# Mixture-of-experts stage of a decoder: turned combination weights copied next to their turning, the routing's exponential at the head of its iteration, the routing in pieces, another tail

## The reference

```python
logits = jnp.einsum('btc,ce->bte', x, router_w) + router_b        # 8 experts
top_k_logits, expert_indices = jax.lax.top_k(logits, 2)
expert_probs = jax.nn.softmax(top_k_logits, axis=-1)
# each token's place in its expert's buffer: a running count over the tokens,
# first choices before second choices; capacity 38 per sequence and expert
einp = buf.at[ei.ravel(), pos.ravel()].add(xr)
h = jnp.einsum('eti,eih->eth', einp2, w_c_fc) + b_c_fc            # 128 -> 512
g = jnp.einsum('eti,eih->eth', einp2, w_gate) + b_gate
o = jnp.einsum('eth,eho->eto', jax.nn.silu(h * g), w_c_proj) + b_c_proj
sel = o[i, p]
return jnp.sum(pr[..., None] * sel, axis=1)                       # two choices, weighted
```

## Time and profile before

| | |
|---|---|
| median of 3 runs | 2416.77 us (2414.82 to 2422.31) |
| the profiled execution: its time / its span | 2416.03 us / 2414.1 us |
| busy share of the span: PE, DVE, ACT, POOL | 76%, 72%, 63%, 51% |
| granted TensorE clock over the span | 0.875 of 2.4 GHz |
| this stage, first `hidden` to the end | 1785.4 to 2414.1 us |

### The profile page before, as it was taken

The page is one execution under the profiler, slowest core; times in us unless marked ns, Lnnn a source line. Parts: engine busy times, 40 slices in busy tenths (PEclk is TensorE's granted clock), DMA queues, the critical chain, the costliest instruction groups (busy, mean ns, idle before and its releaser), DMA issues. The chain is left out here.

```text
span 2414.1 us, 51135 instructions
## 1 busy us (share of the span) xinstructions
PE 1843.7 (76%) x16165; PEld 1336.3 (55%) x16174; DVE 1733.8 (72%) x4027; ACT 1510.8 (63%) x2647; POOL 1236.7 (51%) x1186
## 2 busy tenths in 40 slices
PE   3777777799999824444677499999868898888888
PEld 2556555466666612222345377777646666666665
DVE  5889995689888689998566378888655555545553
ACT  1788886577777645554465477877535556556554
POOL 2656664588888757877666378888610000000000
PEclk7799998699999955555888699999979999999999
DMA  4000000101010030000000000000000000000000
GB/s 137 2 0 0 0 1 2 41 22 31 21 31 21 5 104 1 0 0 1 1 0 0 14 7 8 8 8 1 1 1 10 0 9 9 9 0 9 9 9 9
DMA packets 63117, 32.46 MB, mean 13 GB/s; under 512 B 27737, under 2 KB 59569, under 8 KB 63025
## 3 DMA queue, kind: packets, MB, share of 16 engines
q1 hardware_dynamic: 60576, 30.42, 4.7%
q10 hardware_dynamic: 2448, 0.90, 0.2%
HBM read 27.12 MB, written 4.19 MB: 13 GB/s over the span
## 5 line engine op out<-in xcount | busy, mean ns | idle before, releaser
L3174 DVE SCALAR_TENSOR_TENSOR m_z<-psum,bias_col,m_hb 128x304 f32<-128x304 f32 x256 | 134.4, 532 | 206.8 <-ACT m_hb L3030 199.8
L182 POOL TENSOR_SCALAR mln_ve<-mln_mv 128x4 f32<-128x4 f32 x16 | 4.5, 280 | 484.7 <-DVE mln_mv L149 484.7
L3030 ACT ACTIVATE m_hb<-psum,bias_col 128x304 f32<-128x304 f32 x256 | 130.7, 511 | 171.8 <-PE psum L2929 171.2
L2929 PE MATMUL psum<-m_xt,w_fc 128*128 128x304 f32 x512 | 175.5, 424 | 4.5 <-ACT m_xt L3022 4.5
L1412 POOL TENSOR_TENSOR x_gated<-x_score,x_gate 128x1232 f32<-128x1232 f32 x64 | 168.5, 2632 | 12.7 <-ACT x_score L1347 9.6
L2932 PE MATMUL psum<-m_xt,w_gate 128*128 128x304 f32 x512 | 174.9, 423 | 0.0
L2941 PE MATMUL psum<-m_hid,w_proj 128*128 128x304 f32 x512 | 171.4, 421 | 0.0
L470 POOL TENSOR_SCALAR_AFFINE_SELECT a_prob<-a_prob 128x1024 f32<-128x1024 f32 x128 | 137.5, 1096 | 54.7 <-ACT a_prob L515 54.0
L1354 ACT COPY x_pT<-psum 77x512 f32<-77x512 f32 x256 | 135.8, 581 | 44.8 <-PE psum L1225 43.4
L1419 POOL TENSOR_TENSOR x_gated<-x_gated,x_rden 128x1232 f32<-128x1232 f32 x64 | 143.8, 2247 | 35.8 <-DVE x_rden L1498 30.7
L509 ACT ACTIVATE a_prob<-psum 128x1024 f32<-128x1024 f32 x128 | 129.6, 1029 | 50.3 <-PE psum L619 29.8
(11 more groups left out here) (408 smaller groups left out, 5644.3 us busy)
## 6 DMA issues: line engine op xcount, KB each, us to landing
x_ctx<-in_ctx_dram SPq DMA_DIRECT2D x32, 154.0 KB
x_mask<-in_mask_BxSxS_ik_dram SPq DMA_DIRECT2D x64, 77.0 KB, 2.6
x_resident<-in_x_dram SPq DMA_DIRECT2D x8, 512.0 KB, 7.0
out_dram<-x_resident SPq DMA_DIRECT2D x8, 512.0 KB, 3.2
x_gate<-in_fside_BxSxS_dram SPq DMA_DIRECT2D x16, 154.0 KB, 2.5
w_fc<-in_L_ffn_w_c_fc_dram SPq DMA_DIRECT2D x1, 2048.0 KB, 9.2
w_gate<-in_L_ffn_w_gate_dram SPq DMA_DIRECT2D x1, 2048.0 KB, 14.2
const<-in_const_dram SPq DMA_DIRECT2D x1, 607.0 KB, 6.1
```

The costliest lines, as they stand in the source:

```text
L2929: pe.matmul(psum[:, 2 + k % 2, 0:N * K], core.w_fc[:, e, f * P:(f + 1) * P], rhs, start=True, stop=True).then_inc(sem["h_ps"], PER_STEP)
L3030: act.activation(hb[:, k % 2, :], psum[:, 2 + k % 2, 0:N * K], ACT.Identity, bias=bias[:, fcb + k:fcb + k + 1]).then_inc(sem["h"], PER_STEP)
L3174: dve.scalar_tensor_tensor(out=z[:, k % 2, :], in0=psum[:, 4 + k % 2, 0:N * K], scalar=bias[:, gb + k:gb + k + 1], in1=hb[:, k % 2, :], op ...
```

## The change

Nothing of the arithmetic changes. On ScalarE, `combine_copy(n)` moves from k = 4n + 6, behind `expert_out`, to k = 4n + 4; the exponential moves from k = 24 of the iteration before to the very start of its own iteration; in the tail `slots_copy` runs two sequences ahead of where it was. On TensorE, `dispatch` for sequences 0 and 1 stands ahead of the tail's first `turn_rows`, and the others follow two sequences earlier. On VectorE, `combine(0)` moves from ahead of z(0) to ahead of z(1); the three operations on probabilities move from `finish` to a function of their own behind z(0); statistics are made in two halves, behind z of k = 2 and 3; normalising stands at k = 5 and 6; `choose` is split into `best` (k = 21) and `choose` (k = 22), and `finish` into `finish` (k = 29) and `keys` (k = 30); six instead of four `slots` stand ahead of the first addition. The helper `statistics_of` was there before.

```diff
@@ TensorE, iteration @@
+                if ahead:
+                    dispatch(i + STEP, 0)
+                    dispatch(i + STEP, 1)
                 pe.wait_ge(sem["oT"], i + STEP)
...
                     ins.then_inc(sem["y_ps"], BATCH)
-                    if ahead:
-                        dispatch(i + STEP, n)
+                    if ahead and n + 2 < N:
+                        dispatch(i + STEP, n + 2)
@@ ScalarE, iteration @@
+                chosen_exp(i)
                 first(0)
                 for k in range(STEPS):
                     if k + 1 < STEPS:
                         first(k + 1)
                     silu(k)
+                    if k % NF == 0 and k:
+                        combine_copy(k // NF - 1)
                     if k % NF == 2 and k > NF:
                         expert_out(k // NF - 1)
-                        combine_copy(k // NF - 1)
                     if ahead and k in (10, 14):
                         input_copy(i + STEP, (k - 10) // NF)
-                    if ahead and k == 24:
-                        chosen_exp(i + STEP)
                 expert_out(E - 1)
+                if ahead:
+                    slots_copy(i + STEP, 0)
                 combine_copy(N - 1)
...
+                if ahead:
+                    slots_copy(i + STEP, 1)
                 rows_copy(0)
                 for n in range(N):
                     if n + 1 < N:
                         rows_copy(n + 1)
-                    if ahead:
-                        slots_copy(i + STEP, n)
+                    if ahead and n + 2 < N:
+                        slots_copy(i + STEP, n + 2)
@@ VectorE @@
+            def probabilities(i):
+                prob_chain.start(i)
+                dve.wait_ge(sem["eexp"], i + STEP)
+                prob_chain.link(dve, dve.tensor_scalar(diff[:], ex[:], 1.0, None, ALU.add))
+                prob_chain.link(dve, dve.reciprocal(prob[:, 0, :], diff[:]))
+                prob_chain.last(dve, dve.tensor_tensor(prob[:, 1, :], ex[:], prob[:, 0, :], ALU.mult))
...
                 for k in range(STEPS):
-                    if k % NF == 0:
+                    if k == 1:
+                        combine(0)
+                    if k % NF == 0 and k:
                         combine(k // NF)
...
-                    if ahead and k == 1:
-                        statistics(i + STEP)
-                    if ahead and k in (4, 6):
-                        normalise(i + STEP, (k - 4) // 2)
-                    if ahead and k == 20:
+                    if k == 0:
+                        probabilities(i)
+                    if ahead and k in (2, 3):
+                        statistics(i + STEP, k - 2)
+                    if ahead and k in (5, 6):
+                        normalise(i + STEP, k - 5)
+                    if ahead and k == 21:
+                        best(i + STEP)
+                    if ahead and k == 22:
                         choose(i + STEP)
                     if ahead and k == 29:
                         finish(i + STEP)
+                    if ahead and k == 30:
+                        keys(i + STEP)
                 for s in range(STREAMS):
                     if ahead:
-                        for n in range(s * QUAD, (s + 1) * QUAD):
+                        for n in ((0, 1, 2, 3, 4, 5), (6, 7))[s]:
                             slots(i + STEP, n)
```

More of the change, by code:

```diff
@@ L2844, in moe @@
         chain = Chain(core, "m_chain", STEP)
+        prob_chain = Chain(core, "m_prob_chain", STEP)
         xn = core.sb("m_xn", [P, N, C])
@@ L3072, in iteration @@
                         rows_copy(n + 1)
-                    if ahead:
-                        slots_copy(i + STEP, n)
+                    if ahead and n + 2 < N:
+                        slots_copy(i + STEP, n + 2)
             input_copy(1, 0)
             input_copy(1, 1)
-            chosen_exp(1)
             for n in range(N):
@@ L3095, in _, with statistics, best @@
             link = lambda ins: chain.link(dve, ins)
-            def statistics(i):
-                ln.statistics(dve, i, lambda s, b: core.x_cols(i, s, b))
+            def statistics(i, s):
+                ln.statistics_of(dve, i, s, lambda b: core.x_cols(i, s, b))
             def normalise(i, s):
                 ln.apply(dve, i, s, lambda b: core.x_cols(i, s, b), lambda b: xn[:, s * QUAD + b, :], sem["xn"])
-            def choose(i):
+            def best(i):
                 chain.start(i)
@@ L3115, in choose @@
                 dve.tensor_tensor(diff[:], top[:, :, 1], top[:, :, 0], ALU.subtract).then_inc(sem["diff"], STEP)
+            def choose(i):
                 for n in range(N):
@@ L3138, in finish, with keys @@
                 link(dve.tensor_scalar(idxf[:], idxf[:], float(K), None, ALU.mult))
+            def keys(i):
                 link(dve.tensor_scalar(over[:], pos[:], float(K), -4.0 * P * E, ALU.is_ge, ALU.mult))
@@ L3191, in iteration @@
                     dve.tensor_tensor(x, x, psum[:, 1, :], ALU.add).then_inc(sem["x_out"], UNIT)
-            statistics(1)
+            for s in range(STREAMS):
+                statistics(1, s)
             for s in range(STREAMS):
                 normalise(1, s)
+            best(1)
             choose(1)
             finish(1)
+            keys(1)
             for n in range(N):
```

## The result

The changed kernel takes 2345.91 us, the median of 4 runs (2342.82 to 2346.61), beside 2415.80 for the kernel before in the same comparison (4 runs, 2412.98 to 2422.31). The ratio is 0.9705, with a 95% interval of 0.9683 to 0.9726. The forecast was 2346.5.

A forecast was written before the change was run, and what follows sets the result against it. TensorE was taken to set the time. Terms 68.1 + 8.8 - 9.4 + 0.8 + 1.6 = 69.9 us off 2416.03 gave 2346.1, stated as 2346.5 us; range 2341 to 2351 (68%), widened to 2336 to 2360.

The forecast's parts named there:

- The copies' place: Turnings on TensorE no longer wait for the copy to m_ct: 8.77 us in each of 7 iterations, -68.1 us in all.
- the head: At an iteration's start, TensorE waits for z behind VectorE's moved work: +1.1 us an iteration, +9.4 us in all.
- I cost all these cuts at nothing.: Cutting choose and finish into smaller blocks on VectorE was taken to cost nothing.
- The tail: Last projection's end to next hidden(0): dispatches fill waits, -1.25 us in each of 7 iterations, -8.8 us; 13.6 us left.
- Table loads: Exp's load at the head takes 1.28 us, hidden by the tail; the skill's 2.7 us rule would add some 10 us.
- Ahead of the loop: Before the loop, halved statistics let GpSimd start the first routing 0.8 us earlier: -0.8 us.
- The clock: In the seventh iteration, a stretch of TensorE at 1.2 GHz goes with the 2 us wait before it: -1.6 us.
- the fall at each head: Rival: TensorE's clock falls once in each iteration, after the head's new wait; +13 us, 2359 us; chance 10%.
- the half clock in the tails: Rival: TensorE stays at 1.2 GHz through every tail, 91 us more, 2437 us; chance 3%.
- The turning's wait: Rival: turnings wait on as before; only the surplus of two long waits goes, 14.4 us, giving 2401 us; chance 4%.
- The head was not free: Answers the rival that the head costs nothing because VectorE catches up: 9 us more gained, 2337 us; chance 7%.
- A matrix was late once: Answers the rival that the tail's second dispatch waits up to 0.9 us for its matrix in 7 iterations: 2352 us; 7%.

The follow-up runs named there:

- e2: The changed kernel with combine_copy(n) put back behind expert_out at k = 4n + 6, all else as changed; 2405.37 us, ratio 0.9948.
- e5: The changed kernel with finish and keys in one block behind z(29) again; 2345.58 us, ratio 0.9706, iteration 69.69 us.
- e1: The kernel before with only combine_copy(n) moved to k = 4n + 4; 2358.59 us, ratio 0.9748, iteration 71.17 us.
- e6: e4 with the exponential back at k = 24 of the iteration before and the probabilities back ahead of finish; 2347.48 us, iteration 69.71 us.
- e9: e4 with only the exponential back at k = 24 of the iteration before; 2342.76 us, ratio 0.9692, iteration 69.27 us.
- e4: The changed kernel with combine(0) ahead of z(2), second half of statistics and normalising placed later; 2334.74 us, ratio 0.9659, iteration 68.68 us.

## Why the prediction was right

*The copies' place.* Right in mechanism, place and size. The kernel lost 8.77 us an iteration there by the starts of the earlier trace rows, and no turning waits in the changed kernel. e2 gives the same from the other side, 54.5 us for 56 waits. The loop's gain, 9.15 us an iteration, is 0.2 above my sum. Behind each of the seven waits the turning itself ran 0.01 to 0.02 slower, which I left out, and the 0.17 behind `choose` (under e5) went as well. The last iteration gave 6.0; forecast were 6.7 less the head's 1.1, 5.6.

*"I cost all these cuts at nothing."* True of `finish` (e5), nearly so of `choose`, and the sum needed no more. But the reason that I gave, that ScalarE and VectorE have room on the average, was too easy. e1 shows that the copies alone bring 7.7 an iteration, not 8.8: once TensorE doesn't pause, two table loads, `combine(7)` and `finish` within five steps come through to the last projections. The exponential's and the probabilities' new places are what keeps the 8.77 whole: by e6 and e9, on top of e4, they are worth 0.59 and 0.44. I had seen their cost (the head) and took their gain for part of the sixth wait. The changed kernel's total doesn't depend on which is right, and to that extent its agreement is luck; e1 and e6 depend on it, and there I was wrong by up to 1.1 and 1.0 us an iteration.

*The tail.* 13.64 against a forecast of 13.6. `turn_rows` is 0.17 late instead of 0.83, and no wait for `m_xt` is left in the loop. The matrix for the second dispatch comes out just in time, as forecast, but for the first tail, where it costs 0.32; e9 shows the same in every tail, 0.42 us late.

*The head.* z(1) at h + 4.01 (forecast 4.0), `hidden(3)` at h + 4.60 (4.6), late by 1.02 (0.9 and restart), `hidden(6)` late by 0.23 (0.15); in the first iteration the recorded wait is 0.52 longer (0.6). The first period is 0.84 longer than the others; most of the rest is the late matrix of its tail. The head is a price that the change need not pay: e4 takes 1.01 of it away.

*Table loads.* The page ScalarE: Activation LUTs of the Trainium skill (Rules for kernel authors) would have put 2.7 us on a switch. The section What ACT_TABLE_LOAD costs, which the prediction sets against it, does not differ: its 1283 ns is the load alone, and a drain brings it to 2.66 us. This trace shows the load and no drain: a row of 1.28 us from 1926.53, and the exponential at 1927.83. The load at the head starts 0.81 us before h and lets `first(0)` start at h + 0.72; by the rule, as an estimate from that page, it would have been over a microsecond later. The stage has the 16 loads of the forecast:

```profile
L3022 ACT ACT_TABLE_LOAD x8 | 10.3, 1283 | 0.1
L3041 ACT ACT_TABLE_LOAD x8 | 10.3, 1283 | 0.1
```

*Ahead of the loop.* From the first statistics to the first `hidden(0)` it was 1757.09 to 1785.41, 28.32 us, and is 1759.57 to 1787.13, 27.56: 0.76 less (0.8). The row that does it, GpSimd's first inverse root, starts 1.84 us behind the first statistics where it started 2.61 behind:

```profile
1759.57 0.87 DVE L155 BATCH_NORM_STATS2 mln_stats<-x_resident 128x6 f32<-128x128 f32 x4 [3.09 <-PEq L71]
...
1761.41 1.04 POOL L184 TENSOR_TENSOR mln_rstd<-mln_ve,minus_half 128x4 f32<-128x4 f32 x1
```

*The clock.* The stretch at 1.2 GHz of the earlier trace rows is gone, as forecast. Whether the 2 us wait caused it stays open: seven waits of that length stood in the same trace, and one was followed by such a stretch. None of the twelve traces of kernels without that wait shows one in the loop.

*The rivals.* No window of the loop shows the lower clock, so neither the fall at each head nor the half clock in the tails came. For the latter I had cited the Trainium skill's page TensorE: Matmul & The Clock Gate (PE-mode transpose). The tails lie in windows with a granted clock of 1.00; but this is a weak test of the rule, since I counted wrongly: not half of a tail's matmuls turn, but 3 of 11 for each sequence (3 turnings, 6 for the product, 2 for the dispatch), and they take 0.33 of 1.51 us. The turning's wait went with the copy's place (e1 and e2). The head was not free. A matrix was late once, by 0.32 us in the first tail, and not in 7 iterations. The total agrees better than it should, and that is luck: stage and prologue gained 71.7 us where 69.9 were forecast, and the stages ahead happened to take 2.5 us more in this execution.

## What to carry to other kernels

When the engine that sets the time stops waiting, ask next which block on the others had been catching up in those waits: the first cure gave 7.7 us an iteration instead of 8.8 until the table loads and the block of small operations stood elsewhere. Place what an engine owes to a shared bank right behind the work that fills it, not behind the next output; and where a late and a long instruction share a stretch of few steps, move one to where the other engines have lead. Small effects are read from the period of one iteration, which repeats within 0.03 us here, not from the total, which varies by several us.

## What the runs showed of the hardware

- A start is late by more than the recorded idle time, by nearly the same amount each time: 0.79 recorded and 0.96 by the starts, 0.85 and 1.02, 0.46 and 0.63, 1.99 and 2.15. These 0.16 to 0.17 us are a matter of the record: a product's row is 0.68 long where the next product starts after 0.51. Behind a wait the first product takes some 0.1 us more to its successor (1931.94 to 1932.56, 0.62 instead of 0.51).
- A start can be late without any bracket: 0.23 us at 1937.21, behind z of 1936.62. Only the distance between starts shows it.
- A bracket can name "issue" where the awaited data came last (1911.61 in e9, 1844.63 in the changed kernel).
- The stages ahead of this one, the same in all kernels, took times up to some 10 us apart in the profiled executions (first `hidden(0)` at 1779.7 to 1789.7, both in kernels with the new order ahead of the loop). I didn't look for the cause.
- A change of table is one row of 1283 ns on ScalarE, all 28 times before and all 16 times after.
